# The first group's self attention in two units of two batches, P V halves side by side, feed-forward steps three beats on

## What is computed

```
x = x + attn(layernorm(x))            # linear attention, 16 heads of 8, sigmoid q and k
   h, q, k, v = x@Wh+bh, sigmoid(x@Wq+bq), sigmoid(x@Wk+bk), x@Wv+bv
   attn = q (k^T v) / (q sum k);  gated = LN(attn) * (h + beta);  out = relu(gated @ Wo + bo)
x = x + xattn(layernorm(x), ctx)      # softmax cross attention, 16 heads of 64, then @ Wo + bo
x = x + ffn(layernorm(x))             # shared SwiGLU (width 256) + one of 8 routed experts per token
```

## Time and profile before

| | us |
|---|---|
| median of 3 runs | 674.99 (673.2 to 675.08) |
| the profiled execution | 670.19 |
| its span | 668.5 |
| first scores of the cross attention start (from the span's start) | 48.5 |
| last scores start | 560.24 |
| first tile of the tail | 575.07 |
| PE busy | 604.9 (90%) |
| DVE, ACT, POOL busy | 427.8, 422.2, 308.4 |

### The profile page before, as it was taken

The page is one execution under the profiler, slowest core; times in us unless marked ns, Lnnn a source line. Parts: engine busy times, 40 slices in busy tenths (PEclk is TensorE's granted clock), DMA queues, the critical chain, the costliest instruction groups (busy, mean ns, idle before and its releaser), DMA issues.

```text
span 668.5 us, 14932 instructions
## 1 busy us (share of the span) xinstructions
PE 604.9 (90%) x5231; PEld 511.7 (77%) x5231; DVE 427.8 (64%) x1187; ACT 422.2 (63%) x1510; POOL 308.4 (46%) x331
## 2 busy tenths in 40 slices
PE   2578999999998999899999999999999989799993
PEld 2467888878897889788978898889888867566662
DVE  3758655876577658665866686658654456277562
ACT  2238678667766776667666766676667666244551
POOL 3434553355346433743374328432832435146653
PEclk9879999999999999999999999999999999899997
DMA  6200000000001000100010000000000003625420
GB/s 171 77 17 13 17 2 2 13 17 1 2 21 41 1 1 14 49 1 1 14 50 1 1 14 33 1 2 1 33 1 1 17 17 111 198 61 163 137 76 11
DMA packets 24952, 23.48 MB, mean 35 GB/s; under 512 B 7007, under 2 KB 22497, under 8 KB 24880
## 3 DMA queue, kind: packets, MB, share of 16 engines
q1 hardware_dynamic: 20368, 14.91, 8.1%
q0 software_dynamic: 2784, 6.32, 2.6%
q10 hardware_dynamic: 1728, 1.32, 0.7%
HBM read 15.03 MB, written 7.95 MB: 34 GB/s over the span
## 4 chain that ended last, share of the span: by engine, by line
PE 55%; DVE 13%; POOL 10%; issue 10%; ACT 8%; DMA 3%; SPq 0%; DVEq 0%; POOLq 0%
PE bank L1108 7%; PE bank L1223 7%; PE bank L1255 7%; PE bank L1110 5%; PE bank L1109 5%; PE bank L1233 5%; PE bank L1244 5%; ACT prob L1011 4%; PE bank L1333 4%; POOL routed L533 4%; POOL prob L541 3%; DVE mneg L797 2%; PE bank L1358 2%; PE bank L1115 1%; POOL rstd L482 1%
## 5 line engine op out<-in xcount | busy, mean ns | idle before, releaser
L1011 ACT ACTIVATE prob<-bank,mneg 128x128 f32<-128x128 f32 x512 | 182.8, 382 | 99.9 <-DVE mneg L797 99.8
L541 POOL TENSOR_TENSOR prob<-prob,rden 128x512 f32<-128x512 f32 x128 | 130.7, 1042 | 169.9 <-DVE rden L804 169.8
L1011 ACT ACTIVATION_READ_ACCUMULATOR prob<-bank,mneg 128x1 f32 x512 | 112.8, 220 | 0.0
L1017 ACT COPY probT<-bank 128x512 f32<-128x512 f32 x128 | 77.3, 604 | 46.1 <-PE bank L1233 45.5
L797 DVE TENSOR_REDUCE mneg<-bank 128x4 f32<-128x512 f32 x128 | 81.3, 677 | 27.3 <-PE bank L1223 27.3
L1233 PE MATMUL bank<-ident,prob 128*128 128x128 f32 x512 | 78.1, 275 | 3.0 <-POOL prob L541 3.0
L1223 PE MATMUL bank<-kT,qT 64*128 64x128 f32 x1024 | 74.4, 284 | 6.7 <-ACT qT L1027 3.3
L1223 PEld LDWEIGHTS bank<-kT,qT 64*128 64x128 f32 x1024 | 62.4, 187 | 18.4 <-issue 13.3
L1244 PE MATMUL bank<-probT,V 128*64 128x128 f32 x1024 | 70.7, 281 | 0.0
L482 POOL TENSOR_TENSOR rstd<-var_eps,neg_half 128x4 f32<-128x4 f32 x24 | 24.4, 1018 | 94.4 <-DVE var_eps L634 94.4
L1233 PEld LDWEIGHTS bank<-ident,prob 128*128 128x128 f32 x512 | 60.1, 142 | 9.1 <-issue 4.8
(11 more groups left out here) (194 smaller groups left out, 1330.3 us busy)
## 6 DMA issues: line engine op xcount, KB each, us to landing
prob<-routed SPq DMA_DIRECT2D x39, 128.5 KB, 2.2
xin<-in_x_dram SPq DMA_DIRECT2D x8, 256.0 KB, 3.2
ctx_nat<-in_ctx_dram SPq DMA_DIRECT2D x8, 192.0 KB, 2.5
routed<-blank ACTq DMA_DIRECT2D x8, 128.5 KB
qT<-in_L_ffn_rt_gate_dram SPq DMA_DIRECT2D x1, 1024.0 KB, 8.3
qT<-in_L_ffn_rt_up_dram SPq DMA_DIRECT2D x1, 1024.0 KB, 9.9
out_dram<-probT,prob POOLq DMA_INDIRECT x39, 2.5
prob<-in_L_xattn_Wq_dram SPq DMA_DIRECT2D x1, 512.0 KB, 6.9
```

The costliest lines, as they stand in the source:

```text
L541: nc.gpsimd.tensor_tensor(view, view, spread(rden[:, m % 2, c * NC:(c + 1) * NC], 2, S), ALU.mult)\
L1011: last = nc.scalar.activation(prob[:, m % 2, p * S:(p + 1) * S], bank[c % 2][:, i * S:(i + 1) * S], ACT.Exp, bias=mneg[:, m % 2, p:p + 1], ...
L1017: nc.scalar.copy(probT[:, m % 2, c * 512:(c + 1) * 512], made(r1, ("T", m, c))[:])\
```

## The change

1. `UNITS`: group 0's self attention becomes two units, batches 0-1 and 2-3, with their own starts (`S1_AT` in beats: unit 0 at n = -6 beat 0, unit 1 eleven beats later). Steps of these units work on half the columns or two batches, and need one bank where a whole group needs two. Units 2 to 8 are groups 1 to 7. The loop starts one n later (`FIRST` = -6), so the same steps of unit 0 stand four beats nearer to the first scores. Unit 1's later steps (gating, output, x1, turn x1) stand beside batches 0 and 1 of the cross attention. q of pair 1 is made in beats 2 and 3 of n = 0, two quarters each.
2. Loads: x of group 0 in two DMAs (`x0_in`), the first at the head of SP's queue; Wh, Wk and Wv go to ACT's queue; `bq` has its own semaphore; the context goes ahead of six other loads. POOL builds `head_mask` (8 instructions) before its first `rstd` and before it waits for the bias rows; the context is turned at beat 4.
3. P V: both halves of batch n-1 stand in beat 0 of n, `out_product` and `residual` in beat 2.
4. Feed-forward: `turn h` from (1,0) to (1,3), `logits` (1,1) to (2,0), `gate and up 0` (1,2) to (2,1), `rank` (1,3) to (2,2), `gate and up 1` (3,0) to (4,1), `down` (4,1) to (5,0), and the others with them; group 6's last steps stand in beats 2 and 3 of n = 30 (before: beat 3 of n = 29 and beats 0 and 1 of n = 30).

```diff
-        FIRST, LAST = -7, B
-        S1_AT = [FIRST] + [GB * g - 6 for g in range(1, NG)]
-        F_AT = [GB * g + GB for g in range(NG - 1)]
+        FIRST, LAST = -6, B
+        UNITS = [(0, 0, 2), (0, 2, GB)] + [(g, 0, GB) for g in range(1, NG)]
+        S1_AT = [NC * FIRST, NC * FIRST + 11] + [NC * (GB * g - 6) for g in range(1, NG)]
+        F_AT = [NC * (GB * g + GB) for g in range(NG - 1)]
...
-        PE_F = {(1, 0): "turn h", (1, 1): "logits", (1, 2): "gate and up 0", (1, 3): "rank",
-                (3, 0): "gate and up 1", (4, 1): "down"}
+        PE_F = {(1, 3): "turn h", (2, 0): "logits", (2, 1): "gate and up 0", (2, 2): "rank",
+                (4, 1): "gate and up 1", (5, 0): "down"}
...
-                if b == 1 and live(n - 1):
+                    r1.add(("PV", n - 1, 0), "act")
+                    r1.add(("PV", n - 1, 1), "act")
+                if b == 2 and live(n - 1):
                     r1.add(("out", n - 1), "dve")
-                if b == 2 and live(n):
-                    r1.add(("PV", n, 0), "act")
...
-            load_x(0)
-            sp.dma_start(rawkvh[:, 0:D], Wh).then_inc(w_in, 16)
-            sp.dma_start(rawkvh[:, D:2 * D], Wk).then_inc(w_in, 16)
-            sp.dma_start(rawkvh[:, 2 * D:], Wv).then_inc(w_in, 16)
+            load_first(0)
             sp.dma_start(rawq1, Wq).then_inc(w_in, 16)
-            sp.dma_start(bq_col[:], bq.rearrange("(p o) -> p o", o=1)).then_inc(w_in, 16)
+            sp.dma_start(bq_col[:], bq.rearrange("(p o) -> p o", o=1)).then_inc(bq_in, 16)
             sp.dma_start(rawk, XWk).then_inc(wx_in[0], 16)
+            load_ctx(0)
...
+            act.dma_start(rawkvh[:, 0:D], Wh).then_inc(w_in, 16)
+            act.dma_start(rawkvh[:, D:2 * D], Wk).then_inc(w_in, 16)
+            act.dma_start(rawkvh[:, 2 * D:], Wv).then_inc(w_in, 16)
```

More of the change, by code:

```diff
@@ L308, in decoder_layer @@
                    (3, 1): "residual"}
-        PE_F = {(1, 0): "turn h", (1, 1): "logits", (1, 2): "gate and up 0", (1, 3): "rank",
-                (3, 0): "gate and up 1", (4, 1): "down"}
[L311 to L314, removed]
-        L6 = F_AT[-1]
[L318 to L322, removed]
+        PE_F = {(1, 3): "turn h", (2, 0): "logits", (2, 1): "gate and up 0", (2, 2): "rank",
+                (4, 1): "gate and up 1", (5, 0): "down"}
+        ACT_F = {(1, 3): "copy h^T", (2, 0): "score", (2, 1): "tanh 0", (4, 1): "tanh 1"}
+        DVE_F = {(1, 1): "normalise", (1, 3): "h^T low", (2, 0): "route", (2, 1): "activate 0", (2, 2): "rows",
+                 (4, 1): "activate 1", (5, 0): "shared"}
+        POOL_F = {(0, 3): "rstd", (2, 3): "record", (5, 1): "scatter"}
+        L6 = F_AT[-1]
+        MOVED = {(NG - 2, "gate and up 1"): L6 + 10, (NG - 2, "tanh 1"): L6 + 10, (NG - 2, "activate 1"): L6 + 10,
+                 (NG - 2, "down"): L6 + 11, (NG - 2, "shared"): L6 + 11, (NG - 2, "scatter"): L6 + 11,
+                 (0, "turn context"): S1_AT[0] + 4, (0, "context high"): S1_AT[0] + 4, (0, "context low"): S1_AT[0] + 5}
         def steps_at(table_, starts, n, b):
-            return [(g, step) for g, a in enumerate(starts) for (slot, beat), step in table_.items()
-                    if MOVED.get((g, step), (a + slot, int(beat))) == (n, b)]
+            return [(u, step) for u, a in enumerate(starts) for (slot, beat), step in table_.items()
+                    if MOVED.get((u, step), a + NC * slot + int(beat)) == NC * n + b]
         PE_TAIL = {4: ["turn h"], 5: ["logits"], 6: ["gate and up 0"], 7: ["rank"], 8: ["gate and up 1"],
@@ L343, in decoder_layer, with s1_banks @@
                     "turn x1": [(12, "dve")]}
+        def s1_banks(u, step):
+            if whole(u):
+                return S1_BANKS[step]
+            if step == "project second pair" or (u, step) == (1, "turn context"):
+                return []
+            return S1_BANKS[step][:1] if step in ("k^T v", "q k^T v") else S1_BANKS[step]
         F_BANKS = {"turn h": [("h", "dve")], "logits": [("l", "dve")],
@@ L1119, in s1 @@
                 if step == "turn x":
[L1120 to L1126 removed]
+                    pe.wait_ge(normed[0], u + 1)
@@ new lines, in s1 @@
+                    turned((name, 0), xn, b0, b1)
+                if step == "project first pair" or (step == "project second pair" and whole(u)):
+                    pe.wait_ge(*r2.freed((name, 0)))
+                    for i in ((1, 2) if step == "project first pair" else (3, 4)):
+                        ps = claim(r2, (name, i))
+                        b = b0 + i - 1
+                        product3(ps[:, 0:3 * D], xnT_hi[:, b * S:(b + 1) * S], xnT_lo[:, b * S:(b + 1) * S], wkvh_hi[:],
@@ L1169, in ffn @@
                     pe.wait_ge(h3_in, g + 1)
-                    turned(g, "h", h3)
+                    turned((g, "h"), h3)
                 if step == "logits":
```

377 lines of the change are left out of this document (202 added, 175 removed).

## The result

The changed kernel took 676.84 us (median of 20 runs, 674.47 to 679.23), the kernel before 674.4 us (median of 20 runs, 672.83 to 675.87): ratio 1.0035, 95% interval 1.0023 to 1.0047. It is slower by 0.35%, where I had forecast 665 us. Its profiled execution took 675.39 us with a span of 673.7, where that of before had 670.19 and 668.5.

The account below looks back on a forecast made before the run. PE sets the pace in the middle (busy 65.6 of 67.7 us). Start -4, P V -6.5, feed-forward -9.6 and +9.5, last batches +0.7 sum to -9.9: 670.19 becomes 660.3, plus 4.8 carried over gives 665 us, range 651 to 673.

Parts of the forecast that it names:

- The start: From the loads through batch 0: first scores 7 us sooner, 3 us charged beside batch 0, together -4 us.
- With two batches they take half, 12.6 us less: Chain to the first scores: pieces handling four batches, some 25 us, halve with two; earlier loads give 2 us more.
- Unit 1's 7.5 us: Unit 1's work on PE and DVE between unit 0's output and the first scores delays those scores by 7.5 us.
- Batches 0 to 2: Unit 1's gating, output, x1 and normalisation fall beside batch 0: charged 3 us, between 1.2 and 5.
- Rival (b): The start gives nothing: first scores win 3 us and batch 0 takes them back; 669 us, chance 0.15.
- P V together: Two P V blocks side by side enter and leave once: 0.24 us less PE per batch, -6.5 us in 27 batches.
- Feed-forward later: PE's waits at turn h (4.4 us) and gate and up 0 (5.2 us) go: together -9.6 us.
- The new wait: PE's gate and up 1 waits for DVE's context low to free its bank: 1.9 us in five groups, +9.5 us.
- Last batches and transition: Last scores come 6.5 us sooner, first tail tile 21.5 us after them instead of 14.8: +0.7 us in all.
- The 4.8 us carried over: Distance of the median of three runs above the profiled execution of before, added to 660.3 to give 665 us.
- (c): ACT's chain paces the first halves, so a 0.60 us copy is paid each time: slower, 681 us, chance 0.10.
- (d): The order tables leave the old waits (+9.6 us) and the new one comes too: 674.6 us, chance 0.07.

Follow-up runs that it names:

- experiments 1 and 2: The changed kernel with the loads in the order of before, 675.08 us, ratio 1.0021; and with only the bias rows ahead of the weights on ACT's queue, 676.3 us, 1.004.
- experiment 13: The first kernel of experiments 9 to 11, with group 1's turned x and projections moved behind the first scores: 655.37 us, ratio 0.9689.
- experiment 5: The kernel before with P V halves together, output product and residual in beat 2, and the new feed-forward times; start and loads as before: 669.39 us, ratio 0.9921.
- experiment 14: The first kernel of experiments 9 to 11, with P V halves, output product and residual back where they were before the change: 666.09 us, ratio 0.9862.
- experiment 3: The kernel before with only P V halves together, output product and residual in beat 2: 694.63 us, ratio 1.0309.
- experiments 9 to 11: In order: changed kernel with old start and three table steps moved, 0.9649; changed kernel, unit 1 seven beats sooner, 1.0062; kernel before, P V halves paired only, 1.0167.
- experiment 12: The changed kernel with unit 1 started 7 beats sooner and the loads in the order of before: 674.76 us, ratio 0.9999.

## Why the prediction was wrong, step by step

**The start: the step that failed** (-7 and +3 forecast, +1.2 and +5.2 measured, 10.4 us off in the trace). All three of its terms were off: the halving of the chain with the loads by 10.0 us, batches 0 to 2 by 2.2, and unit 1 by 1.7 the other way.
- *"With two batches they take half, 12.6 us less", and 2 more for the loads.* Unit 0's chain came 4.6 us sooner, not 14.6. Ahead of hkv it waited for loads in whatever order they stood (experiments 1 and 2): PE's q k^T v started at 22.21 us for 21.24, later than before, though x was there 3.0 us sooner. From there to the turn of x1 it took 12.0 us, where before it took 16.6: the pieces did not halve (two statistics 0.49 us, four 0.87) and between them stand things that don't depend on the batches, such as POOL's rstd and the 1.22 us of `xwq_lo` between gating and x1.
- *Unit 1's 7.5 us.* Measured, 5.8 us between x1's turn and the first scores (14.0 for 8.2). This term was right in kind. But the first scores are not behind unit 0's chain alone: in the order of PE the q pieces, group 1's turned x and one projection stand between, in both kernels. Moving these didn't help in the kernel without units (experiment 13).
- *Batches 0 to 2, "I charge 3 us, between 1.2 and 5".* 5.2 us, beyond the far end, and 5.6 against experiment 5. I added up unit 1's busy time. What decides is where it stands in DVE's order. In batch 1 of the changed kernel DVE worked from 57.08 to 73.5 us without a gap:

```profile
62.79 0.60 DVE L673 TENSOR_SCALAR h<-x,mv,rstd 128x128 f32<-128x128 f32 x2
...
66.52 1.24 DVE L833 TENSOR_REDUCE mneg<-bank 128x4 f32<-128x512 f32 x2
67.67 3.11 DVE L732 SCALAR_TENSOR_TENSOR attn<-attn,mv,hw 128x128 f32<-128x128 f32 x4
```

  The row maxima of the scores of 63.26 us came at 66.52; POOL's probabilities came late as well, T waited 2.38 us at 68.73 and the next scores 1.26 us. The granted clock was at its lower level for both:

```profile
68.73 1.09 PE L1286 MATMUL bank<-ident,prob 128*128 128x128 f32 x4 [2.38 <-POOL prob L574]
71.08 2.08 PE L1276 MATMUL bank<-kT,qT 64*128 64x128 f32 x16 [1.26 <-ACT prob L1055]
```

  From 64 to 72 us PE was busy for 4.4 of 8 us at a mean clock of 0.76 (the rows beside experiment 5). T took 1.09 us where 0.60 is usual, and the scores 2.08 for 1.16: the lower level. In experiment 5, where the row maxima came at 62.95 us, the clock of the same stretch was 1.00. The clock was below 1.00 (0.95) in the 14 us before too, so the late row maxima are not all of the loss; what keeps it lower there was not followed.

  Rival (b) named two of these (small instructions don't halve, bias rows hold the gating) and DVE's 9.9 of 12.6 us as evidence, and I gave it 0.15 and priced it at no gain, not at a loss.

**P V together** (-0.24 us a batch). Right in sign, too small: 0.49 a batch with the waits out of the way (experiment 14), of which PE's busy time is 0.30. I had looked at the entry and the exit of one block in one place, and I took for granted that it can be had by itself. On the feed-forward's old table it can't (experiments 3 and 11).

**Feed-forward later.** The two waits of the earlier trace rows went. The new wait was forecast at 1.9 us five times and was 1.52 five times; the steps behind it in PE's order paid it in full, as I had said. What I missed is the scatters: I wrote that they "have some 3 us before POOL's next normalisation is wanted". They stand ahead of POOL's normalisation in beat 2, and T waited 1.27 to 1.44 us for it, five times. The period came out at 66.9 as forecast by luck: PE's busy time fell by 1.7 us where the 0.96 of P V was forecast, the context wait was 0.4 shorter, and the missed wait 1.3 worse. A sum that agrees is no proof of its terms.

**Last batches and transition.** -6.3 for -6.5, and the first tile 22.09 us after the last scores for 21.5. POOL's timeline shows the chain, as the prediction had it, with the clock at 0.85:

```profile
565.78 1.01 POOL L566 DMA_INDIRECT routed<-record,row_i  x1 [5.50 <-DVEq L829]
...
570.63 2.04 POOL L574 TENSOR_TENSOR prob<-prob,rden 128x512 f32<-128x512 f32 x2
```

**The 4.8 us carried over, and the tail.** I added the distance between the profiled execution of before and the median, without knowing what it was. Most of it is probably a stall at tiles 14 to 20 of the tail. In the profiled execution of before these six tiles took 10.4 us, in that of the changed kernel 15.4, and in eleven of the experiments 13.6 to 16.6. PE's timeline there:

```profile
611.11 0.27 PE L1380 MATMUL bank<-ident,prob 128*128 128x128 f32 x1
...
613.36 0.44 PE L1402 MATMUL bank<-ident,V 128*128 128x128 f32 x2 [1.12 <-issue]
615.56 0.71 PE L1411 MATMUL bank<-kT,V 128*128 x4 [1.76 <-DVE probT L993]
```

The three kernels of experiments 9 to 11 ran on a chip that no other experiment ran on, beside the kernel before at 669.5 us, which is 4 to 6 us below its time beside the others, and in each of the three these tiles took 10.4 us. The other eleven ran on three more chips, and all have the stall. So it may belong to the chip, but there is no kernel with a trace from two of them that would show it. So I read the stall as part of most timed runs of before too, though not of its profiled execution; the timed runs have no trace that would show it. Of the 5.2 us between the profiled executions the tail has 3.4: 5.0 of stall, less 1.6 elsewhere in it that I didn't follow. The medians, with the stall presumably in both, differ by 2.4. It was right to carry the 4.8 us, but by luck.

**Rivals (c) and (d).** ACT's chain did not pace the first halves: in the changed kernel's middle PE waits for exp 0.25 us a period. (d), "the waits stay, the new one comes too", gave 674.6 and is near the time, for another reason: the waits went.

## What to carry to other kernels

A step of a hand-written order has a price only together with the order around it: two parts that cost 21 and 9 us alone gained 5 together, and the two waits that were left each went with one step of a table moved. After such a change look for the waits that are new, not only for the old ones that went; each of two here was worth over 1%. Work split off to shorten a chain lands beside other work, and what it costs there is read from the in-order queue that it stands in, ahead of a row maximum or a normalisation, not from the busy share; a wait that lowers the clock costs more than its own length.

## What the runs showed of the hardware that I had not expected

- The last of four broadcast rows of 64 KB on ACT's queue landed 11.4 us after its issue, behind three weights and while SP's queue was loading too; with the rows first and alone on that queue the sum on POOL started at 9.19 us, where it had started at 15.17.
- A few microseconds of waits cost more than themselves: after a stretch with PE busy for 8.99 of 11.29 us the granted clock was 0.77 over the next 11.7 us (experiment 3), and after a wait of 2.38 us T took 1.09 us for 0.60.
- The first half of DVE's gating (four records) took 1.14 us in the first group of before, with no normalisation on POOL, 2.05 us where its first 1.37 us lay beside POOL's normalisation (392.46 us, before), and 3.11 us where 1.96 us did (67.67 us in the changed kernel). Its records took 0.34 us each alone and 1.07 to 1.13 beside POOL.
- The stall at tiles 14 to 20: ACT and DVE stood for 1.7 to 2.4 us with a releaser that the profile doesn't know. It was absent in the three traces from one chip and there in the eleven from three others. Its cause was not found and stays open.
- Open too: why the clock is below 1.00 in the changed kernel's first 14 us of cross attention, when PE is busy for 13.8 of them. With unit 1 sooner and the loads of before (experiment 12) it is 1.00 in the same stretch.
